# First attention of a graph network: gather indices kept on chip, query rows loaded by SyncE, edge attributes in pairs of groups

## The chip, the cores and the metric

The kernel runs on one NeuronCore of a Trainium2 chip. Its engines are TensorE (PE, with its weight loads PEld), VectorE (DVE), ScalarE (ACT), GpSimd (POOL) and SyncE (SP); each has an instruction queue of its own, and SP, ACT and POOL issue DMAs, which 16 DMA engines carry out. The metric is the device time in microseconds. All arithmetic is in fp32 unless said otherwise.

## The reference, cut to what matters

Four message-passing layers on one graph of 3125 nodes, 64 features and 100,000 edges that are sorted by `dst`, each followed by a residual addition and a layernorm. The change lies in the first one and in its preparation:

```python
Qh, Kh, Vh = (x @ Wq.T + bq), (x @ Wk.T + bk), (x @ Wv.T + bv)     # 3125 x 64, 4 heads of 16
Ee = edge_attr @ We.T + be                                         # 100000 x 64
score = (Kh[src] * Qh[dst] * (1 / sqrt(16)) * Ee).sum(-1)          # per edge and head
score = exp(clip(score, -5, 5))
wV = segment_sum(Vh[src] * score, dst)
x = layernorm(x + wV)
```

## The kernel before, in words

**Tiling.** Edges are cut into G = 98 groups of ST = 1024: 128 partitions (P) by C = 8 columns, partition p of group g holding the edges 8p to 8p+7 of the group. The last group has 84 partitions (PL). Since edges are sorted by `dst`, the destinations of a group fall into a window of W = 64 nodes from a base that is worked out on the chip; a group's rows of queries are fetched with one window and spread to the edges by a one-hot matrix.

**Prologue (L248 to L465).** SyncE and ScalarE load the inputs. `dst_i` (L275, L276) holds every group's destinations in the group layout, so its load is made of pieces of 8 values, 32 bytes. VectorE turns them to fp32 (L370), subtracts each group's base and keeps them as `dst_rel0`. TensorE turns the edge lists (L441), x (L422) and the lowest destinations (L450), and projects x on the weights of K, V and Q: `multiply(k)`, 13 of them, each waiting for ScalarE's copy of the one two before (L315, L316). Among them stands the matmul that spreads the base of every group to all partitions (L459), for which VectorE waits ahead of L378. After the last copy, SyncE stores the K and V rows (`kv_tab`, L287) and ScalarE the Q rows (`q_tab`, L319) to DRAM; the block ends when both have landed.

**First attention (L597 to L857).** One sweep over the 98 groups. Rings of RS = 4 slots hold the gathered K and V rows (`kv`), the edge attributes (`ea`), the indices (`idx`) and the queries (`qwin`). The semaphore `slot_free` starts at 4 and goes up by one with each step's last VectorE instruction (L735). Per step of one group:

- SyncE (`load`, L606) waits for `slot_free`, then loads 4 KB of indices (L544) and 256 KB of edge attributes (L615).
- GpSimd (L630 to L638) issues 8 indirect DMAs, each of 128 rows of 512 bytes from `kv_tab` by one column of `idx`. After the fifth of a group it waits for the indices of the next group (`indices(g + 1)`).
- ScalarE (`front`, L754, and `step`, L777) takes the exponent of the score (L779), then for the next group reads its base into a register and issues two DMAs of 64 query rows into two halves of `qwin` (L761), whose other halves stay zero, copies two transposes out of PSUM (L763, L765), and makes the one-hot of the low part of `src` (L769, L775), for the counting of edges that later layers use.
- TensorE (`step`, L828) counts (L836), turns edge attributes (L794) and one-hots (L802), sums the messages by destination (L851), and multiplies the next group's edge attributes (L811, L813) and queries (L819).
- VectorE (`step`, L690) multiplies keys, edge terms and queries (L704, L712), reduces to the score (L714, L716), adds the counts (L698), makes the one-hots (L676, L683) and the messages (L725), and adds the sum to `acc` (L735).

Each engine's order is written out by hand in these functions; a front half for the next group is woven into each step. The semaphores of the loads count 16 for each finished DMA, whichever number of engines carries it.

After this come a three-hop layer, an attention by matmul, and a last attention with 334 further indirect DMAs on GpSimd (L2282). The change doesn't touch their code.

Of the kernel before, what the change touches and what calls it, by code (L numbers as in the profile page):

```python
# [10 lines left out]
P = 128  # L11
# [55 lines left out]
def build(nc, x, src, dst, edge_attr_2, edge_attr_64, Wq, bq, Wk, bk, We, be, Wv, bv,  # L67
          attn_w, W_fc, W_attn, W_edge, W_e2n, W_m1, W_m2, out):
    ctx = ExitStack()
    with ctx:  # L70
# [86 lines left out]
        g_edge = sb("g_edge", [P, RS, C, D + 4])  # L157
        hot = sb("hot", [P, C, W])
# [27 lines left out]
        def sb(name, shape, dt=fp32):  # L186
# [23 lines left out]
        dst_i = sb("dst_i", [P, G, C], i32)  # L210
# [17 lines left out]
        s_stored = short_sem("tables_stored")  # L228

        early_sems = [s_zero, s_graph, s_gtail, s_x, s_xtail, s_w, s_const, s_edges, s_rest, s_rows, s_tiles, s_flat, s_wt, s_wcopied, s_base, s_basec,  # L230
                      s_bdiag, s_brep, s_sp, s_spt, s_turned, s_copied, s_done, s_taken, s_ones, s_stored]
# [12 lines left out]
        by_pool, by_dve = free_at + 5000, free_at + 7500  # L244

        XT0 = [range(t, min(t + MT, NT)) for t in range(0, NT, MT)]
        MM0 = [range(t, min(t + 2, NT)) for t in range(0, NT, 2)]
        with nc.Block() as block:  # L248
# [12 lines left out]
            def _(sp):  # L261
# [13 lines left out]
                sp.dma_start(dst_i[:, 0:G - 1, :], dst[0:full].rearrange("(g p c) -> p g c", p=P, c=C)).then_inc(s_edges, 16)  # L275
                sp.dma_start(dst_i[0:PL, G - 1, :], dst[full:E].rearrange("(p c) -> p c", c=C)).then_inc(s_edges, 16)  # L276
# [47 lines left out]
            def _(dve):  # L324
                nc.vector.memset(dst_i[:, G - 1, :], int(NONE))
# [43 lines left out]
                dve.wait_ge(s_edges, 32)  # L369
                nc.vector.tensor_copy(dst_rel0[:, :, :], dst_i[:, :, :])  # L370
# [7 lines left out]
                nc.vector.tensor_copy(group_base[:, :], bank[1][:, :])  # L378
                dve.drain()
# [33 lines left out]
                nc.vector.tensor_scalar(tile_hiw[:, :, :], tile_hi[:, :, :], float(WC), 1.0, ALU.mult, ALU.add)  # L413

            @block.tensor
            def _(pe):
# [8 lines left out]
                def multiply(k):  # L425
# [5 lines left out]
                    last.then_inc(s_done, 1)  # L431

# [22 lines left out]
                for k in range(4):  # L455
                    multiply(k)
# [4 lines left out]
                for k in range(4, len(MM0)):  # L461
                    multiply(k)
# [66 lines left out]
        def pass_on(eng):  # L529

            eng.sem_inc(passed, 1)
# [20 lines left out]
        qwin = sb("qwin", [P, RS, 2, D])  # L552
# [33 lines left out]
        slot_free, idx_in = short_sem("a_slot_free"), [short_sem(f"a_idx{s}") for s in range(RS)]  # L586
        ea_in, kv_in = [short_sem(f"a_ea{s}") for s in range(RS)], [short_sem(f"a_kv{s}") for s in range(RS)]
        hot_ok, ea_t, ea_ts, hot_t, hot_ts = short_sem("a_hot"), short_sem("a_eaT"), short_sem("a_eaTs"), short_sem("a_hotT"), short_sem("a_hotTs")
        ee_ok, qd_ok, sc_ok, ex_ok, msg_ok, sum_ok = (short_sem("a_ee"), short_sem("a_qd"), short_sem("a_score"), short_sem("a_exp"), short_sem("a_msg"), short_sem("a_sum"))
        cleared, q_in = short_sem("a_cleared"), short_sem("a_queries")  # L590
# [3 lines left out]
        loop_sems = [begun, slot_free, *idx_in, *ea_in, hot_ok, ea_t, ea_ts, hot_t, hot_ts, ee_ok, qd_ok, sc_ok, ex_ok, msg_ok, sum_ok,  # L594
                     cleared, q_in, key_ok, lo_ok, count_ok, bank_free, count_clear]
        nc.clear_and_free_semaphores(early_sems)
        with nc.Block() as block:  # L597
# [23 lines left out]
            def _(pool):  # L621
                nj = sweeps(pool, 1)
                with pool.Fori(0, nj) as j:
# [7 lines left out]
                    for g in range(G):  # L631
                        s = g % RS
                        for c in range(C):
# [3 lines left out]
                            if c == C // 2 and g + 1 < G:  # L637
                                indices(g + 1)  # L638
# [2360 lines left out]
```

## Time and profile before

| | us |
|---|---|
| median of 3 runs | 1912.07 |
| lowest and highest | 1908.1, 1912.09 |
| span of the profiled execution | 2674.2 |
| prologue, up to the first instruction of the attention's block | 47.2 |
| first gather, last gather issued | 51.75, 1442.83 |
| first gather of the last attention | 1818.4 |

The page gives no time around the span of the profiled execution. The span is from its first to its last instruction, and is longer than the time of the runs. Busy shares of the span: PE 56%, PEld 47%, DVE 53%, ACT 38%, POOL 46%.

How to read a group of instructions: line, engine, operation, tiles written and read, shapes, count; then busy time in us and mean ns of one; then the idle time of the engine right before them, and what ended it. "remote" is a semaphore event that the profile ties to no instruction that had just ended, "issue" is none at all. "PEld" is TensorE's weight load. A "q" behind an engine is its sequencer, which issues DMAs.

### The profile page before, as it was taken

The numbers are of one execution on the slowest core, as the hardware profiler recorded it, in microseconds if no ns is written. First come the engines' busy times: TensorE is split into PE (matmuls) and PEld (weight loads), VectorE is DVE, ScalarE is ACT, GpSimd is POOL, SyncE is SP. The second block draws the span as 40 slices with busy tenths as digits, with TensorE's granted clock in tenths as the row PEclk, the third lists the DMA queues.
The fourth block names the chain that finished last, engine by engine and source line by source line (L and its number), as shares of the span: only waits on it lengthen the run. The fifth ranks groups of instructions, "written<-read, shape, count | busy, mean of one in ns | idle before, by whom it ended". The sixth has DMA issues, their size and how long they took to land. (4 is left out here: it accounts for less than half of the span.)

```text
span 2674.2 us, 43621 instructions
## 1 busy us (share of the span) xinstructions
PE 1501.4 (56%) x12903; PEld 1250.3 (47%) x12903; DVE 1423.4 (53%) x3785; ACT 1008.8 (38%) x2221; POOL 1227.4 (46%) x1328
## 2 busy tenths in 40 slices
PE   3555555555555654555555774754134656555795
PEld 2444444434444443344434673753033645444785
DVE  6455555555555554555555787871023534434685
ACT  3333333333333333333333651750003534434683
POOL 2555555555555554545553460546724343444100
PEclk7677777777777767777777787885556777777897
DMA  5222222222222222222221210022201111111100
GB/s 116 54 58 56 58 59 57 59 57 61 57 58 60 56 59 52 60 55 58 59 57 35 62 59 3 2 87 34 35 17 33 37 34 37 32 41 33 40 26 14
DMA packets 125233, 128.69 MB, mean 48 GB/s; under 512 B 80959, under 2 KB 88435, under 8 KB 124840
## 3 DMA queue, kind: packets, MB, share of 16 engines
q0 software_dynamic: 35776, 62.74, 10.4%
q1 hardware_dynamic: 63778, 57.41, 7.8%
q10 hardware_dynamic: 25542, 6.81, 1.1%
q8 instruction: 75, 1.23, 0.2%
q14 instruction: 62, 0.51, 0.1%
HBM read 116.64 MB, written 10.20 MB: 47 GB/s over the span
## 5 line engine op out<-in xcount | busy, mean ns | idle before, releaser
L634 POOL DMA_INDIRECT shared<-kv_tab,idx x784 | 763.2, 974 | 674.3 <-DMA idx<-in_src 459.3
L836 PE MATMUL bank<-key_hot,lo_hot 128*128 128x350 f16 x784 | 220.8, 394 | 586.5 <-DVE count L698 392.4
L836 PEld LDWEIGHTS bank<-key_hot,lo_hot 128*128 128x128 f16 x784 | 59.3, 101 | 703.4 <-issue 690.4
L2282 POOL DMA_INDIRECT count<-att_tab,count x240 | 228.3, 951 | 301.7 <-PE bank L2827 193.4
L698 DVE TENSOR_TENSOR count<-count,bank 128x350 f32 x392 | 205.4, 524 | 109.4 <-issue 73.6
L735 DVE TENSOR_TENSOR acc<-acc,bank 65x64 f32 x98 | 21.3, 217 | 429.2 <-remote 425.8
L779 ACT ACTIVATE expo<-score 128x32 f32<-128x32 f32 x98 | 22.5, 229 | 587.3 <-DVE score L716 566.9
L769 ACT ACTIVATE lo_dist<-iota_neg,tile_lo 128x128 f16<-128x128 f32 x784 | 238.5, 389 | 0.0
L2656 ACT ACTIVATE shared<-shared 128x126 f32<-128x126 bf16 x336 | 144.4, 484 | 172.0 <-PE bank L2804 88.6
L683 DVE TENSOR_SCALAR key_hot<-iota_key,tile_key 128x350 f16<-128x350 f16 x784 | 193.3, 319 | 0.0
L851 PEld LDWEIGHTS bank<-hots,msg 128*65 128x65 f32 x1568 | 183.8, 221 | 0.4 <-DVE msg L725 0.4
L2804 PE MATMUL bank<-shared 128*128 128x150 f32 x896 | 154.1, 319 | 48.2 <-DVE shared L2509 22.6
L851 PE MATMUL bank<-hots,msg 128*65 128x64 f32 x1568 | 180.4, 303 | 0.0
L2804 PEld LDWEIGHTS bank<-shared 128*128 128x128 f32 x896 | 137.9, 208 | 70.0 <-issue 61.9
L2770 PE MATMUL bank<-shared,ad_row 128*128 128x25 bf16 x1344 | 67.3, 177 | 180.2 <-issue 174.7
L2516 DVE TENSOR_TENSOR count<-count,bank 128x500 f32 x112 | 74.9, 669 | 172.4 <-remote 154.7
L811 PE MATMUL bank<-webd,eaT 128*128 128x128 f32 x784 | 146.3, 345 | 4.2 <-ACT eaT L763 3.5
L2770 PEld LDWEIGHTS bank<-shared,ad_row 128*128 128x128 bf16 x1344 | 51.7, 99 | 196.4 <-issue 195.5
L2838 PE MATMUL bank<-count,tab 128*68 128x88 f32 x1400 | 134.3, 265 | 6.6 <-DVE count L2516 6.5
L811 PEld LDWEIGHTS bank<-webd,eaT 128*128 128x128 f32 x784 | 133.9, 257 | 4.8 <-ACT eaT L763 3.7
L2282 POOL DMA_INDIRECT g_edge<-att_tab,count x94 | 89.0, 946 | 98.6 <-PE bank L2827 71.1
L2838 PEld LDWEIGHTS bank<-count,tab 128*68 128x68 f32 x1400 | 129.9, 162 | 8.6 <-DVE count L2516 8.3
(528 smaller groups left out, 3237.8 us busy)
## 6 DMA issues: line engine op xcount, KB each, us to landing
shared<-in_edge_attr SPq DMA_DIRECT2D x97, 256.0 KB
shared<-lo_tab SPq DMA_DIRECT2D x28, 512.0 KB
shared<-kv_tab,idx POOLq DMA_INDIRECT x784
count<-att_tab,count POOLq DMA_INDIRECT x240
qwin<-q_tab ACTq DMA_DIRECT2D x196, 16.0 KB
kv_tab<-count SPq DMA_DIRECT2D x1, 1600.0 KB, 10.4
idx<-in_src SPq DMA_DIRECT2D x97, 4.0 KB, 1.6
g_edge<-att_tab,count POOLq DMA_INDIRECT x94
```

The costliest lines, as they stand in the source:

```text
L634: nc.gpsimd.indirect_dma_start(kv[:, s, c, :], None, kv_tab, bass.IndirectOffsetOnAxis(ap=idx[:, s, c:c + 1], axis=0)).then_inc(kv_in[s], 16)
L683: last = nc.vector.tensor_scalar(key_hot[:, c, :], iota_key[:, :], keys[:, c:c + 1], None, ALU.is_equal)
L698: nc.vector.tensor_tensor(at, at, bank[6 + q % 2][:, 0:KC].rearrange("p (h w) -> p h w", w=WC), ALU.add).then_inc(bank_free, 1)
L769: nc.scalar.activation(lo_dist[:, c, :], iota_neg[:, :], ACT.Abs, bias=los[:, c:c + 1])
L811: nc.tensor.matmul(bank[3][:, q * P:(q + 1) * P], eaT[:, q * P:(q + 1) * P], webd[:, :], start=q == 0, stop=False, skip_group_check=True)
L836: last = nc.tensor.matmul(bank[6 + q % 2][:, 0:KC], lo_hot[:, c, :], key_hot[:, c, :], start=i == 0, stop=i == GT - 1)
L851: last = nc.tensor.matmul(bank[5][0:D + 1, 0:W], msg[:, c, :], hots[:, s % 2, c, :], start=c == 0, stop=c == C - 1)
L2282: nc.gpsimd.indirect_dma_start(ring[s][:, j, 0:D + 2], None, att_tab[1], bass.IndirectOffsetOnAxis(ap=src_i[:, t:t + 1], axis=0)).then_inc ...
L2656: nc.scalar.activation(low_w[:, n % LOW_RING, 0:FREE], low_dist[:, n % LOW_RING, 0:FREE], ACT.Relu, bias=p, scale=minus_p).then_inc(low_ok, 1)
L2770: last = nc.tensor.matmul(bank[0][:, t * NT:(t + 1) * NT], lo_turned[:, s, t, :], u_parts[:, k, :], start=k == 0, stop=k == 2)
L2804: nc.tensor.matmul(into[:, 0:NT * QW].rearrange("p (h w) -> p h w", w=QW)[:, :, bass.ds(at[j], TW)], low_w[:, n % LOW_RING, :], keys_w[:, ...
L2838: last = nc.tensor.matmul(sum_of[0:D + 4, 0:UW], tab[:, h, 0:D + 4], blocks[:, i % 2, h, :], start=h == 0, stop=h == NT - 1, skip_group_ch ...
```

## The change

The index ring and the waits for it go. In the prologue `dst` and `src` are each loaded as 98 rows of 1024 values, one group to a partition (`dst_g`, `src_g`; 97 rows in one DMA, the rest in another), made fp32 by VectorE, turned by TensorE in 8 transposes each (`turn_groups`), and copied by VectorE to `dst_rel0` and, as integers, to `idx_all`, which lies in memory that the first attention doesn't use (`g_edge`). GpSimd gathers by columns of `idx_all` and waits for `slot_free` ahead of each group. SyncE loads a step's 64 query rows to both halves of the partitions (`q_raw`); ScalarE copies each half to its place in a single `qwin`. Two groups' edge attributes come in one DMA, except for the last two groups.

```diff
-        dst_i = sb("dst_i", [P, G, C], i32)
+        dst_g, dst_gf = sb("dst_g", [P, ST], i32), sb("dst_gf", [P, ST])
...
+        def turned_groups(b):
+            return bank[b][:, 0:C // 2 * G].rearrange("p (c g) -> p c g", c=C // 2)
...
             @block.sync
-                sp.dma_start(dst_i[:, 0:G - 1, :], dst[0:full].rearrange("(g p c) -> p g c", p=P, c=C)).then_inc(s_edges, 16)
-                sp.dma_start(dst_i[0:PL, G - 1, :], dst[full:E].rearrange("(p c) -> p c", c=C)).then_inc(s_edges, 16)
+                for into, of in ((dst_g, dst), (src_g, src)):
+                    sp.dma_start(into[0:G - 1, :], of[0:full].rearrange("(g e) -> g e", e=ST)).then_inc(s_edges, 16)
+                    sp.dma_start(into[G - 1:G, 0:E - full], of[full:E].rearrange("(a e) -> a e", a=1)).then_inc(s_edges, 16)
...
             @block.vector
-                nc.vector.memset(dst_i[:, G - 1, :], int(NONE))
+                nc.vector.memset(dst_g[:, :], int(NONE))
+                nc.vector.memset(src_g[:, :], 0)
...
-                dve.wait_ge(s_edges, 32)
-                nc.vector.tensor_copy(dst_rel0[:, :, :], dst_i[:, :, :])
+                dve.wait_ge(s_edges, 64)
+                nc.vector.tensor_copy(dst_gf[0:G, :], dst_g[0:G, :])
+                nc.vector.tensor_copy(src_gf[0:G, :], src_g[0:G, :])
+                dve.drain().then_inc(s_dstg, 1)
                 dve.wait_ge(s_basec, 1)
...
                 nc.vector.tensor_copy(group_base[:, :], bank[1][:, :])
+                dve.wait_ge(s_dstt, 1)
+                for k in range(2):
+                    nc.vector.tensor_copy(dst_rel0[:, :, k * C // 2:(k + 1) * C // 2], turned_groups(2 + 5 * k).rearrange("p c g -> p g c"))
...
+                dve.wait_ge(s_srct, 1)
+                for k in range(2):
+                    nc.vector.tensor_copy(idx_all[:, k * C // 2:(k + 1) * C // 2, :], turned_groups(3 + k))
...
             @block.tensor
-                for k in range(4):
+                for k in range(2):
+                    multiply(k)
+                pe.wait_ge(s_dstg, 1)
+                turn_groups(dst_gf, 2, 7, s_dstt)
+                for k in range(2, 4):
                     multiply(k)
                 pe.wait_ge(s_bdiag, 1)
...
-                for k in range(4, len(MM0)):
+                for k in range(4, 6):
+                    multiply(k)
+                turn_groups(src_gf, 3, 4, s_srct)
+                for k in range(6, len(MM0)):
                     multiply(k)
...
             @block.sync
+                    def load_queries(g, s):
+                        b = spans(sp, g)
+                        sp.dma_start(q_raw[:, s, :], q_tab[bass.ds(b, W), :].rearrange("(a w) f -> a w f", a=1).to_broadcast([2, W, D])).then_inc(q_in[s], 16)
+
                     def load(g, s, m):
...
+                        if both and s % 2 == 0:
+                            sp.wait_ge(slot_free, j * G + g + 2)
+                            pass_on(sp)
+                            sp.dma_start(ea[:, s:s + 2, :], ea_main[bass.ds(g, 2), :, :].rearrange("g p n -> p g n")).then_inc(ea_in[s // 2], 16)
...
+                        load_queries(g, s)
+
+                    sp.wait_ge(begun, j + 1)
+                    pass_on(sp)
                     each(sp, load)
             @block.gpsimd
-                    indices(0)
                     for g in range(G):
                         s = g % RS
+                        pool.wait_ge(slot_free, j * G + (g + 1))
+                        pass_on(pool)
                         for c in range(C):
                             nc.gpsimd.indirect_dma_start(
-                                kv[:, s, c, :], None, kv_tab, bass.IndirectOffsetOnAxis(ap=idx[:, s, c:c + 1], axis=0)
+                                kv[:, s, c, :], None, kv_tab, bass.IndirectOffsetOnAxis(ap=idx_all[:, c, g:g + 1], axis=0)
                             ).then_inc(kv_in[s], 16)
-                            if c == C // 2 and g + 1 < G:
-                                indices(g + 1)
             @block.scalar
-                        b = spans(act, g)
+                        act.wait_ge(q_in[s], (j * uses(s) + m) * 16)
+                        pass_on(act)
                         for i in range(2):
-                            act.dma_start(qwin[i * W:(i + 1) * W, s, i, :], q_tab[bass.ds(b, W), :]).then_inc(q_in, 16)
+                            last = nc.scalar.activation(qwin[i * W:(i + 1) * W, i, :], q_raw[i * W:(i + 1) * W, s, :], ACT.Copy)
+                        last.then_inc(q_put, 1)
             @block.tensor
-                        pe.wait_ge(q_in, n * 32)
+                        pe.wait_ge(q_put, n)
```

## Rows read from the trace of the kernel before

**Rows 1.** Page, part 5 (columns as in the section above): three groups of the first attention.

```profile
L634 POOL DMA_INDIRECT shared<-kv_tab,idx x784 | 763.2, 974 | 674.3 <-DMA idx<-in_src 459.3
...
L735 DVE TENSOR_TENSOR acc<-acc,bank 65x64 f32 x98 | 21.3, 217 | 429.2 <-remote 425.8
L779 ACT ACTIVATE expo<-score 128x32 f32<-128x32 f32 x98 | 22.5, 229 | 587.3 <-DVE score L716 566.9
```

**Rows 2.** Timeline: start us, length us, engine, line, tiles, count, [idle before <-releaser].

```profile
616.50 0.60 ACT L763 ACTIVATE eaT<-bank 128x512 f32<-128x512 f32 x1 [1.68 <-issue]
...
618.08 1.93 PE L851 MATMUL bank<-hots,msg 128*65 128x64 f32 x16
...
623.19 0.22 DVE L735 TENSOR_TENSOR acc<-acc,bank 65x64 f32 x1 [2.57 <-remote]
...
623.63 0.33 SPq L544 DMA_DIRECT2D idx<-in_src  x1
...
626.08 0.95 POOL L634 DMA_INDIRECT shared<-kv_tab,idx  x1 [4.29 <-DMA idx<-in_src]
```

**Rows 3.** Timeline of the last steps of the first attention.

```profile
1442.83 0.95 POOL L634 DMA_INDIRECT shared<-kv_tab,idx  x1 [0.30 <-issue]
...
1454.02 0.21 DVE L735 TENSOR_TENSOR acc<-acc,bank 65x64 f32 x1
...
1463.15 0.21 DVE L735 TENSOR_TENSOR acc<-acc,bank 65x64 f32 x1
...
1465.04 0.76 PE L836 MATMUL bank<-key_hot,lo_hot 128*128 128x350 f16 x4 [1.40 <-ACT lo_hot L775]
...
1466.02 0.53 DVE L698 TENSOR_TENSOR count<-count,bank 128x350 f32 x1
```

**Rows 4.** Windows: stretch, its us, busy of PE, PEld, DVE, ACT, POOL, clock, DMA.

```profile
51.70:1443.80 1392.10, 763.08 (x4688) 588.61 (x4688) 744.65 (x1838) 476.30 (x1153) 763.25 (x784) 0.73 0.23 58
```

**Rows 5.** Line L2282: ns min/median/max, first to last start us, forms.

```profile
L2282 POOL DMA_INDIRECT count<-att_tab,count x240: 942/947/1498, 1818.4 to 2425.4; - x120
L2282 POOL DMA_INDIRECT g_edge<-att_tab,count x94: 942/947/994, 1919.4 to 2497.4; - x94
```

**Rows 6.** Timeline of the prologue and of the attention's start.

```profile
5.45 0.40 SPq L275 DMA_DIRECT2D dst_i<-in_dst  x1
...
7.47 2.14 DVE L340 MEMSET count<- 128x2500 int32 x1 [0.47 <-issue]
...
13.62 4.68 PE L441 MATMUL bank<-ident,count 128*128 128x128 f32 x21
...
23.42 0.57 DVE L370 CAST dst_rel<-dst_i 128x784 f32<-128x784 int32 x1
...
24.73 0.39 ACT L315 ACTIVATE count<-bank 128x256 f32<-128x256 f32 x1 [1.67 <-PE bank L430]
...
34.57 0.22 ACT L316 ACTIVATE shared<-bank 128x64 f32<-128x64 f32 x1
...
48.20 2.73 DVE L648 MEMSET count<- 128x3200 int32 x1 [10.77 <-issue]
...
51.75 1.14 POOL L634 DMA_INDIRECT shared<-kv_tab,idx  x1 [45.56 <-DMA idx<-in_src]
```

**Rows 7.** Waits of SyncE's queue, 600 to 1200 us: total us, times, longest.

```profile
SPq L531 <- DVE acc L735: 519.5, 40, 20.5
```

**Rows 8.** DMA queues (packets, MB, share of 16 engines): 2667:2675, 1425:1436, 600:1200.

```profile
q1 hardware_dynamic: 1350, 0.34, 17.0%
...
q1 hardware_dynamic: 196, 0.17, 6.5%
...
q10 hardware_dynamic: 6720, 1.38, 1.1%
```

**Rows 9.** DMA: all packets of 48.1:50, then GpSimd's queue of 600:1200.

```profile
DMA packets 257, 0.76 MB, mean 398 GB/s; under 512 B 16, under 2 KB 16, under 8 KB 257
...
q0 software_dynamic: 10752, 22.04, 14.7%
```

More of the change, by code:

```diff
@@ L157, in build @@
         g_edge = sb("g_edge", [P, RS, C, D + 4])
+        edge_words = g_edge[:, :, :, :].rearrange("p s c f -> p (s c f)")
+        idx_all = edge_words[:, 0:G * C].bitcast(i32).rearrange("p (c g) -> p c g", c=C)
+        src_g, src_gf = edge_words[:, 0:ST].bitcast(i32), edge_words[:, ST:2 * ST]
         hot = sb("hot", [P, C, W])
@@ L431, in multiply, with turn_groups @@
                     last.then_inc(s_done, 1)
+                def turn_groups(of, first, second, turned):
+                    for c in range(C):
+                        last = nc.tensor.transpose(bank[first if c < C // 2 else second][:, c % (C // 2) * G:(c % (C // 2) + 1) * G],
+                                                   of[0:G, :].rearrange("g (p c) -> g c p", c=C)[:, c, :], ident[0:G, 0:G])
+                    last.then_inc(turned, 1)
                 pe.wait_ge(s_const, 4)
@@ L604, in _ @@
                     pass_on(sp)
+                    def load_queries(g, s):
+                        b = spans(sp, g)
+                        sp.dma_start(q_raw[:, s, :], q_tab[bass.ds(b, W), :].rearrange("(a w) f -> a w f", a=1).to_broadcast([2, W, D])).then_inc(q_in[s], 16)
                     def load(g, s, m):
[L607 to L615 removed]
+                        both = not isinstance(g, int)
+                        if both and s % 2 == 0:
+                            sp.wait_ge(slot_free, j * G + g + 2)
+                            pass_on(sp)
+                            sp.dma_start(ea[:, s:s + 2, :], ea_main[bass.ds(g, 2), :, :].rearrange("g p n -> p g n")).then_inc(ea_in[s // 2], 16)
+                        elif not both:
+                            sp.wait_ge(slot_free, j * G + g + 1)
+                            pass_on(sp)
+                            if g == G - 1:
+                                sp.dma_start(ea[0:PL, s, :], ea_last).then_inc(ea_end, 16)
+                            else:
+                                sp.dma_start(ea[:, s, :], ea_main[g, :, :]).then_inc(ea_in[s // 2], 16)
+                        load_queries(g, s)
+                    sp.wait_ge(begun, j + 1)
+                    pass_on(sp)
                     each(sp, load)
@@ L789, in turn_edges @@
                     def turn_edges(g, s, m):
-                        pe.wait_ge(ea_in[s], (j * uses(s) + m) * 16)
+                        if isinstance(g, int) and g == G - 1:
+                            pe.wait_ge(ea_end, (j + 1) * 16)
+                        else:
+                            pe.wait_ge(ea_in[s // 2], (j * ea_loads[s // 2] + m) * 16)
                         pass_on(pe)
```

35 lines of the change are left out of this document (13 added, 22 removed).

## Prediction

> **What bounds the kernel now.** I read the page first, for the span and the engines. The profiled execution spans 2674.2 us, while the median of the runs is 1912.07 us: it is 762 us longer. Its rows give durations and order, but its steps are longer than those of a plain run, so I price the change from rows and add it to the median.
>
> The groups of the first attention come next [rows 1]. GpSimd issues 784 gathers (98 steps of 8), 974 ns each, and idled 459 us for the index load; VectorE idled 426 us ahead of its last addition (L735); ScalarE idled 567 us for VectorE's score. Everybody waits for somebody, so the timeline of one step must say who is last. There [rows 2] TensorE's matmuls of L851, whose semaphore releases L735, end at 620.0, yet L735 starts at 623.2: the release came 3 us after the work. Once the last gather is out, at 1443.8, this lag is gone: L735 stands at 1454.02 and at 1463.15 [rows 3], a step of 9.1 us, against 14.2 us for the mean of the 98 steps of the gather stretch, 1392.1 us long [rows 4]. The late release goes with gathers in the profiled execution.
>
> How long is a step in a plain run? If it were 14.2 us, 98 steps would leave 520 of 1912 us. But the last attention alone issues 334 gathers of 947 ns [rows 5], 0.30 us apart like those of [rows 3]: 418 us. And the stretches without gathers are 52 us ahead of the first [rows 6], 375 us from 1443.8 to 1818.4 and 176 us behind the last [rows 5]. That doesn't fit. GpSimd's own pace nearly does: 8 x (0.974 + 0.30) = 10.2 us a step, 999 us in all, and the sum is 52 + 999 + 375 + 418 + 176 = 2020 us, within 6% of the median. So I take **GpSimd's issue of gathers, 10.2 us a step**, as the bound, with the chain over VectorE and TensorE, 9.1 us, close behind. The 4.3 us that GpSimd waits for indices in the profiled step [rows 2] are an effect, not a cause: the index load of 623.63 was itself let go by L735. GpSimd is three groups ahead there and waits for room.
>
> **The parts in the loop.** *Indices kept on chip.* 98 loads of 4 KB leave SyncE's queue. GpSimd waits for the free slot ahead of a group instead of for the indices after the fifth gather of the group before: one wait for one wait, and the 8 gathers cost the same. When GpSimd sets the pace neither wait stops it. Gain per step: 0, with 0.3 us to either side as bounds, one gap between gathers.
>
> *Query rows.* ScalarE loses two DMA issues and a register load (together with the slot's wait, 1.68 us ahead of L763, [rows 2]) and gets two copies of 64 columns, by the nearest row 0.22 us each [rows 6], 0.45 together: 1.2 us less on ScalarE. But ScalarE idles 5.8 us a step for the score (567 / 98, [rows 1]), and the copy that follows (L763, done at 617.1) is used behind L851, which ends at 620.0 [rows 2]. Value 0; if that cover were gone, the saving would be the 1.2 us. SyncE gets a register load and an issue of about 0.33 us as L544's [rows 2], and nothing is behind it: its queue waited for L735 for 520 of 600 us [rows 7].
>
> *Edge attributes.* One load of 512 KB for two groups starts a step later than now, still three steps, 27 us, ahead of use. An index load needed 2.4 us from issue to use (623.63 to 626.08, [rows 2]); the larger load adds 1.3 us at 398 GB/s [rows 9]. Hidden by two steps.
>
> *Start of the loop.* The first gather starts at 51.75, released by an index load; VectorE, which frees the slots, starts at 48.20 [rows 6]. The gather would then start near 48.4: **3.3 us less**, which counts in full if GpSimd sets the pace. SyncE now waits for the base rows before it loads edge attributes, so step 0 begins later by a load, 2.4 to 3.7 us; GpSimd has four groups of room then, 41 us, and doesn't notice.
>
> **The prologue.** This is where the time moves. The load of dst in 12,416 pieces of 32 bytes becomes two loads, of dst and of src, each of 97 rows of 4096 bytes into 97 partitions. VectorE waits for both ahead of its casts, and TensorE, in the middle of the projections, waits for the casts.
>
> How many of the 16 DMA engines carry such a load? Count packets [rows 8]. At the end of the kernel SyncE's queue stores 1280 rows and then 53 rows of 256 bytes, and shows 1350 packets: 1280 + 53 leaves 17, a closing packet for each of 16 engines and *one* for the 53 rows. The last index and edge loads, of 84 rows each, show 196: 2 x 84 + 2 x 14. ScalarE's 84 loads of 64 rows show 6720: 84 x (64 + 16). So 64 rows take 16 engines, 84 take 14, 53 take one: the largest number up to 16 that divides the rows. 97 is prime, as 53 is: **one engine** carries each load, and the second queues behind the first.
>
> The Trainium skill, DMA: Bandwidth & Descriptors, section "Why a DMA increments its semaphore by 16 and not by 1", states such a rule (the number must divide the slowest dimension of both sides) and, for another way of issuing, an exception that spreads 127 partitions over all engines. By the rule the sum is the one below, by the exception rival A's; no row here has 97 partitions.
>
> Rate of one engine: where large packets run alone, 398 GB/s by 16, or 24.9 GB/s, so 397 KB take 16.0 us; by the gathers' packets, 22.04 MB in 14.7% of 16 x 600 us, 15.6 GB/s and 25.5 us [rows 9]. I take the first: these are plain contiguous rows with the engine nearly to themselves. Two memsets of 1024 columns, 0.88 us each by 2.14 for 2500, stand ahead of SyncE's tail loads, so the first load is issued at 5.45 + 1.7 = 7.15 [rows 6]; two loads take 32.0; with 2.4 from issue to use, the casts start at 41.6. VectorE arrives there at 23.4 and doesn't wait now.
>
> From there: two casts of 1024 columns, 0.74 each by 0.57 for 784, to 43.1; eight transposes at 0.22 (4.68 for 21), to 44.9; the first projection, 0.75, and ScalarE's copies of the 11 projections left, 0.77 each (13 between 24.73 and 34.79, base matmuls included), 8.5; the eight transposes of src, 1.8, of which 0.3 hides behind those copies: 55.7. Now the copies end at 34.8 [rows 6]. The store of the tables follows as now. So **+20.9 us**. VectorE's own work behind the base matmuls (8.8 us, plus four copies of 392 columns) stays beside the stores.
>
> Sum: 1912.1 + 20.9 - 3.3 + 98 x 0 = **1930 us**. Bounds: with 25.5 us a load, +19, 1949; with no wait for the loads at all, the casts (less L370) and the transposes remain, 0.9 + 3.6 - 3.3 = +1, 1913. Both ends are kept.
>
> **Rivals.** *A, the loads are spread* over many engines (10%). Against it, the packet counts. Then it is 1913, or slightly less, since 12,416 small packets no longer stand beside the weights: no change.
>
> *B, the step is set by ScalarE's part* and falls (15%, faster). The place is from the exponent to the one-hots (L779 to L775), for which TensorE's count matmul waits. If this is last in a plain run, each step gains up to 1.2 us, 118 us in all: 1812. It decides from 17.6/98 = 0.18 us a step on; with 0.3 us it is 1900. Against it: in the tail, without any lag, L836 waits for L775 until 1465.04, but VectorE's addition that needs it starts at 1466.02, right behind VectorE's own work [rows 3]. And a faster chain gains nothing while GpSimd needs 10.2.
>
> *C, the wait for indices is a real stall* (5%, faster). The 459 us are 4.7 a step; a tenth of them would give 1884. Against it: the slot's release let the load go.
>
> *D, the loop gets slower* (4%): the double edge load is late once in two steps, 1 us each time, 1979. It decides only if 3.7 us don't fit into three steps.
>
> **How the numbers follow.** The forecast has 66% and 1913 to 1949 as its own range. The range given, 1893 to 1949, adds A and the near part of B and leaves out the rest of B, C and D. About 0.2%, 4 us, is what a measurement of this kernel can tell from no change. Faster: B and C, 0.20. Same: A, 0.10. Slower: the forecast and D, 0.70.
>
> **What the profile after would show.** VectorE idle some 17 us ahead of the casts, released by a DMA; TensorE idle between the second and third projection; the stores issued near 56; the first gather near 69; GpSimd waiting for L735's line where it waited for the index load; a tail step near 9 us. It would be wrong if the casts stood before 30, or if the 8 gathers of a step took less than 10 us. If the median falls though the prologue grew, a plain run's step was not set by GpSimd.

## The result, and the profile after

| | median us | lowest to highest | runs |
|---|---|---|---|
| before | 1912.02 | 1908.1 to 1923.3 | 6 |
| after | 1928.84 | 1918.53 to 1934.17 | 6 |

The ratio of after to before is 1.0076, 95% interval 1.0049 to 1.0103: 16.8 us slower by the medians, where 17.6 us (1930) were forecast. The ratios in this document come from the single runs and aren't the quotient of the two medians (1.0088 here).

The page of after, first line of its head and three groups of the first attention. The first and the third answer to [rows 1]; the second is VectorE's multiplication by the gathered keys. The line numbers have moved (L634 is L676, L704 is L744, L779 is L821, L735 is L775).

```profile
span 1916.7 us, 43354 instructions
...
L676 POOL DMA_INDIRECT shared<-kv_tab,g_edge x784 | 763.0, 973 | 303.1 <-issue 300.9
...
L744 DVE TENSOR_TENSOR prod<-bank,shared 128x512 f32<-128x512 f32 x98 | 67.8, 692 | 135.8 <-DMA shared<-kv_tab,g_edge 116.6
...
L821 ACT ACTIVATE expo<-score 128x32 f32<-128x32 f32 x98 | 22.5, 229 | 217.0 <-DVE score L756 180.1
```

This profiled execution took 1918.53 us, the lowest of its six. Its span fits its time, as the 2674.2 us of the kernel before did not. Of GpSimd's 303.1 idle us 64.4 lie ahead of its first gather, 2.1 us in seven waits for VectorE's L775, and the rest is the 0.30 us between one gather and the next; VectorE waits for the gathers' DMA. So GpSimd is the engine that ends last in the loop. The waits for index loads and for L735 that filled [rows 1] are gone, and the experiments show that they had been peculiar to that one execution.

The prologue of after, from the timeline (start us, length us, engine, line, names, idle before and releaser). It answers to [rows 6].

```profile
7.07 0.42 SPq L284 DMA_DIRECT2D dst_g<-in_dst  x1
7.54 4.49 SPq L285 DMA_DIRECT2D dst_g<-in_dst  x1
...
12.06 0.90 SPq L284 DMA_DIRECT2D g_edge<-in_src  x1
...
13.01 15.06 SPq L285 DMA_DIRECT2D g_edge<-in_src  x1
...
41.77 0.69 DVE L380 CAST dst_gf<-dst_g 98x1024 f32<-98x1024 int32 x1 [17.37 <-DMA g_edge<-in_src]
42.38 0.69 DVE L381 CAST g_edge<-g_edge 98x1024 f32<-98x1024 int32 x1
...
43.16 1.57 PE L454 MATMUL bank<-ident,dst_gf 98*128 98x98 f32 x8 [16.71 <-DVEq L382]
...
56.55 0.22 ACT L325 ACTIVATE shared<-bank 128x64 f32<-128x64 f32 x1
...
56.80 0.42 SPq L296 DMA_DIRECT2D kv_tab<-count  x1
...
70.20 2.73 DVE L688 MEMSET count<- 128x3200 int32 x1 [9.22 <-issue]
...
70.60 1.14 POOL L676 DMA_INDIRECT shared<-kv_tab,g_edge  x1 [64.44 <-issue]
```

VectorE stands idle for 17.37 us until the load of src has landed, and TensorE for 16.71 us behind it. The store of the tables is issued at 56.80, right behind ScalarE's last copy at 56.55; in [rows 6] that copy stands at 34.57. The first gather starts at 70.60, against 51.75.

What the DMA engines moved in that wait, from 14 to 41 us of after, in 40 equal slices: busy tenths of 16 engines, then GB/s.

```profile
DMA  0000000000000000000000013000000111010000
GB/s 24 30 24 24 30 24 24 30 24 24 24 30 24 24 24 30 24 22 30 24 24 30 24 25 33 24 24 24 30 24 24 31 45 49 35 43 24 30 24 24
```

33 of the 40 slices show 24 to 30 GB/s, nearly all with a busy share under a tenth. One engine of 16 is 6% of them, and the prediction's estimate of its rate was 24.9 GB/s. That fits both loads going through one engine, one behind the other; the experiments test it.

### The profile page after: what moved, and what is told of

Read it like the earlier page. It is cut to its first block and busy times, and to the rows that moved or that the text cites. A ratio compares the mean times of both kernels' runs of the same rounds, so it can differ in the third digit from the quotient of the medians.

```text
span 1916.7 us, 43354 instructions
## 1 busy us (share of the span) xinstructions
PE 1357.8 (71%) x12919; PEld 1149.2 (60%) x12919; DVE 1419.6 (74%) x3791; ACT 1069.7 (56%) x2417; POOL 1239.5 (65%) x1328
## 3 DMA queue, kind: packets, MB, share of 16 engines
q0 software_dynamic: 35776, 62.74, 13.7%
## 5 line engine op out<-in xcount | busy, mean ns | idle before, releaser
L676 POOL DMA_INDIRECT shared<-kv_tab,g_edge x784 | 763.0, 973 | 303.1 <-issue 300.9
L881 PE MATMUL bank<-key_hot,lo_hot 128*128 128x350 f16 x784 | 189.0, 347 | 295.1 <-DVE count L738 200.9
L2849 PE MATMUL bank<-shared 128*128 128x150 f32 x896 | 158.0, 325 | 22.2 <-DVE shared L2530 17.6
L744 DVE TENSOR_TENSOR prod<-bank,shared 128x512 f32<-128x512 f32 x98 | 67.8, 692 | 135.8 <-DMA shared<-kv_tab,g_edge 116.6
L807 ACT ACTIVATE hotT<-bank 128x512 f32<-128x512 f32 x98 | 58.5, 597 | 176.4 <-PE bank L847 176.4
L896 PE MATMUL bank<-hots,msg 128*65 128x64 f32 x1568 | 151.3, 270 | 0.0
L896 PEld LDWEIGHTS bank<-hots,msg 128*65 128x65 f32 x1568 | 150.9, 187 | 0.4 <-DVE msg L765 0.4
L821 ACT ACTIVATE expo<-score 128x32 f32<-128x32 f32 x98 | 22.5, 229 | 217.0 <-DVE score L756 180.1
L817 ACT ACTIVATE lo_hot<-lo_dist,small 128x1024 f16<-128x1024 f16 x98 | 112.5, 1148 | 25.4 <-issue 25.3
L2883 PE MATMUL bank<-count,tab 128*68 128x88 f32 x1400 | 112.1, 240 | 9.3 <-DVE count L2561 9.1
L2883 PEld LDWEIGHTS bank<-count,tab 128*68 128x68 f32 x1400 | 107.5, 140 | 11.9 <-DVE count L2561 11.8
L864 PE MATMUL bank<-qwin,hotT 128*128 128x128 f32 x784 | 113.5, 288 | 0.0
```

The costliest lines, as they stand in the source:

```text
L676: nc.gpsimd.indirect_dma_start(kv[:, s, c, :], None, kv_tab, bass.IndirectOffsetOnAxis(ap=idx_all[:, c, g:g + 1], axis=0)).then_inc(kv_in[ ...
L864: last = nc.tensor.matmul(bank[4][:, c * D:(c + 2) * D], hotT[:, c // 2, :], qwin[:, :, :].rearrange("p a f -> p (a f)"), start=True, stop ...
L881: last = nc.tensor.matmul(bank[6 + q % 2][:, 0:KC], lo_hot[:, c, :], key_hot[:, c, :], start=i == 0, stop=i == GT - 1)
L896: last = nc.tensor.matmul(bank[5][0:D + 1, 0:W], msg[:, c, :], hots[:, s % 2, c, :], start=c == 0, stop=c == C - 1)
L2849: nc.tensor.matmul(into[:, 0:NT * QW].rearrange("p (h w) -> p h w", w=QW)[:, :, bass.ds(at[j], TW)], low_w[:, n % LOW_RING, :], keys_w[:, ...
L2883: last = nc.tensor.matmul(sum_of[0:D + 4, 0:UW], tab[:, h, 0:D + 4], blocks[:, i % 2, h, :], start=h == 0, stop=h == NT - 1, skip_group_ch ...
```

## The experiments

Twelve experiments were run, on ten edited kernels; one of these and the kernel before were each run a second time. The kernel before ran beside each of the four batches: 1912.69, 1910.75, 1912.32 and 1912.14 us median.

### The loads cut into 96 rows and one

```diff
-sp.dma_start(into[0:G - 1, :], of[0:full]...)
+sp.dma_start(into[0:G - 2, :], of[0:full - ST]...)
+sp.dma_start(into[G - 2:G - 1, :], of[full - ST:full]...)
-dve.wait_ge(s_edges, 64)
+dve.wait_ge(s_edges, 96)
```

> The changed kernel, but each of the two long loads is cut into 96 rows and one row, so that 96 rows can go over 16 DMA engines. Theory (one engine carried the 97 rows): both loads land before VectorE asks for them near 24.4 us, its 17.4 us of idle time ahead of the casts vanish, and of the prologue's growth only casts and transposes stay: about 17 us less than the changed kernel, 1912 +-4. Rival (the loads are slow for their bytes or for their 4096-byte rows, not for the number of engines): the casts stay near 41 us and the time near 1929.

1907.14 us (12 runs), ratio to before 0.9978, interval 0.996 to 0.9996: 21.7 us less than after. The timeline:

```profile
7.07 0.43 SPq L284 DMA_DIRECT2D dst_g<-in_dst  x1
...
7.54 0.26 SPq L285 DMA_DIRECT2D dst_g<-in_dst  x1
...
24.48 0.69 DVE L381 CAST dst_gf<-dst_g 98x1024 f32<-98x1024 int32 x1
...
36.89 0.22 ACT L326 ACTIVATE shared<-bank 128x64 f32<-128x64 f32 x1
...
50.93 1.14 POOL L677 DMA_INDIRECT shared<-kv_tab,g_edge  x1 [44.77 <-issue]
```

The same bytes, cast and turned by the same instructions, now cost no wait: the casts start as soon as VectorE is free, 17.3 us earlier than in after, the last copy 19.7 and the first gather 19.7 us earlier. 97 rows in one load are the cause of the loss, and the casts and the transposes are not; that it isn't the loop is shown below. SyncE's queue, blocked for 4.49 and 15.06 us in after, is free at once.

It came out 5 us below the 1912 that were expected, just outside the 4 us allowed, so it ran again later:

> The version whose loads are cut into 96 rows and one row, a second time: it measured 0.998 of before. By the prediction's own sum without the wait it should be 1 us over before, 1912; if the 3.6 us below were real, 1907 again. Theory: first gather 0.9 us earlier than before and the rest the same, so 1909 to 1911, ratio 0.998 to 1.000; rival: 1905 to 1908, ratio under 0.998.

1906.87 us (12 runs), ratio 0.9975, interval 0.9962 to 0.9988: again 5 us below before, on the rival's side of what I had written. The version is faster than both kernels. Where its 5 us come from is taken up with the clock, below.

### One of the two loads only

```diff
+if of is dst:
     sp.dma_start(into[0:G - 1, :], ...)
+else:
+    sp.dma_start(into[0:G - 2, :], ...)
+    sp.dma_start(into[G - 2:G - 1, :], ...)
-dve.wait_ge(s_edges, 64)
+dve.wait_ge(s_edges, 80)
```

> Only dst is still loaded as 97 rows; src is cut into 96 rows and one row. Theory (each 97-row load takes one engine for 16.0 us, and the second queued behind the first): issued at 7.1, a load of 16.0 us and up to 2 us for what else that engine carries end at 25 to 27, the casts start at 25 to 27.5 instead of 24.5 (both cut) and 41.8 (none cut), and the time is 1 to 3 us over the version with both cut, 1908 to 1911. Rival (the two loads do not add, each is slow in itself because of its waiting or its issue, which blocked SyncE): casts at 41, time 1927 to 1930. SyncE should be blocked by no issue for more than 5 us.

1914.82 us (12 runs), ratio 1.002, interval 1.0005 to 1.0035. The timeline of its casts:

```profile
28.05 0.69 DVE L384 CAST dst_gf<-dst_g 98x1024 f32<-98x1024 int32 x1 [3.17 <-DMA g_edge<-in_src]
```

The casts start 3.4 us later than with both loads cut (24.65 in its twin, the second run of the version above, in the same batch) and 13.7 us earlier than with none cut. So the two loads do add, and the rival, that each is slow in itself, falls. SyncE's longest issue took 4.42 us, behind the load of dst, as expected under 5. The casts came 0.5 us after the end of the bracket. The releaser named is src, so the rows of src that fall to the engine of dst probably queue behind it; that wasn't tested by itself. The time was 4 to 7 us above what I expected. The first gather stood 6.3 us later than in the twin (57.37 against 51.10), though the casts were only 3.4 us late. The windows from 29 to 35 us, this kernel first and then its twin, show the rest (stretch, its us, busy of PE, PEld, DVE, ACT, POOL, granted clock, DMA share, GB/s):

```profile
29.00:35.00 6.00, 5.57 (x24) 5.57 (x25) 1.91 (x6) 1.11 (x4) 0.00 (x0) 0.55 0.01 3
29.00:35.00 6.00, 6.00 (x40) 5.40 (x40) 4.72 (x9) 3.37 (x13) 0.00 (x0) 1.00 0.02 4
```

TensorE had stood idle for 2.50 us ahead of the transposes of dst, and did the work behind them at a granted clock of 0.55 instead of 1.00: 8 projections took 2.82 us instead of 1.49, and the base matmuls 1.92 instead of 1.06.

### The new prologue with the old loop

The kernel before, with the loads, casts, transposes and memsets of after; src is turned, but the loop loads its indices as before.

```diff
-sp.dma_start(dst_i[:, 0:G - 1, :], ...)
+for into, of in ((dst_g, dst), (src_g, src)):
+    sp.dma_start(into[0:G - 1, :], ...)
...
+turn_groups(dst_gf, 2, 7, s_dstt)
...
+turn_groups(src_gf, 3, 4, s_srct)
```

> The kernel before with the new prologue alone: both long loads, casts, transposes and copies as in the change, but the loop loads its indices, queries and edge attributes as before (the turned indices are made and not used). Theory (all of the loss is in the prologue, the loop gives back only its earlier first gather): 21 to 22 us over the kernel before, 1933, that is 3 to 4 us over the changed kernel. Rival (the loop part of the change costs or saves something per step): the difference to the changed kernel is clearly other than 3 to 4 us, by 98 times what a step gained or lost.

1930.34 us (6 runs), ratio 1.0111, interval 1.0078 to 1.0144. That is 1.5 us over after, within the spread of both, where 3 to 4 were expected. The prologue holds the whole loss. The gathers of this kernel and of after, by line (ns min/median/max, first to last start us):

```profile
L666 POOL DMA_INDIRECT shared<-kv_tab,idx x784: 940/944/2202, 73.9 to 1075.2; - x196
```

```profile
L676 POOL DMA_INDIRECT shared<-kv_tab,g_edge x784: 940/944/2322, 70.6 to 1071.2; - x196
```

The part of the change in the loop lets the gathers start 3.3 us earlier, as predicted, and then both kernels need the same time for them: 1001.3 and 1000.6 us, 10.2 us for a step of 8.

### Two sweeps instead of one

One line in either kernel makes the whole loop run twice, so the difference to the kernel of one sweep is the price of a loop without its prologue.

```diff
-nc.vector.tensor_scalar(sweeps_i[:, 1:2], sweeps_f[:, 2:3], 1.0, None, ALU.add)
+nc.vector.tensor_scalar(sweeps_i[:, 1:2], sweeps_f[:, 2:3], 2.0, None, ALU.add)
```

> The kernel before with one more sweep over all 98 groups in the first attention, which adds nothing to the sums. Its extra time, divided by 98, is the length of a step in a plain run. Theory (GpSimd's issue sets the pace, 10.2 us): 1000 to 1030 us more, with the sweep's own start in it. Rival C (the wait for indices is a real stall of 4 us a step): 1390 us more. Rival B (ScalarE's part decides): 1000 to 1120, and clearly more than the same edit gives to the changed kernel.

> The changed kernel with one more sweep over all 98 groups of the first attention, which adds nothing to the sums. Theory (GpSimd's issue of 784 gathers sets the pace before and after): the extra time is the same as the extra sweep's in the kernel before, to within 10 us (0.1 us a step), 1000 to 1030. Rivals B and C: it is less than before by up to 118 or by up to 400 us. If SyncE's later loads slow a step down, it is more.

2932.32 us (before) and 2945.58 us (after), 4 runs each: a sweep costs 1019.6 and 1016.7 us more than one sweep did. The loop of after is 2.9 us cheaper over 98 steps, 0.03 us a step, which the measurement can't tell from nothing. The gathers of the two kernels, by line:

```profile
L634 POOL DMA_INDIRECT shared<-kv_tab,idx x1568: 940/944/2202, 51.8 to 2071.9; - x196
```

```profile
L676 POOL DMA_INDIRECT shared<-kv_tab,g_edge x1568: 940/945/2310, 75.6 to 2094.5; - x196
```

2020.1 and 2018.9 us for 1567 intervals are 1.289 and 1.288 us each, with the pause between the sweeps in them.

### Half of the gathers

The pace of the gathers could hide a gain in the rest of the step. So each step gathers only for the first four of its eight chunks of edges; the output leaves out the other half of the edges.

```diff
-for c in range(C):
+for c in range(C // 2):
     nc.gpsimd.indirect_dma_start(
...
-dve.wait_ge(kv_in[s], m * (16 * C))
+dve.wait_ge(kv_in[s], m * (8 * C))
```

> The kernel before with 4 of 8 gathers in each step of the first attention; half of the keys and values are zeros, so its output leaves out half of the edges. GpSimd then needs 5.1 us a step, and what is behind it shows. Theory: the chain over VectorE and TensorE, 9.0 to 9.5 us a step, becomes the bound: 70 to 115 us under 1912, so 1797 to 1842. If a step takes no less time, GpSimd was not the bound.

> The changed kernel with 4 of 8 gathers in each step of the first attention; its output leaves out half of the edges. Theory: again 9.0 to 9.5 us a step. ScalarE's saved 1.2 us a step is off the chain, so it stands 14 to 22 us over the same edit on the kernel before, the prologue's loss (a little more than in the full kernel, since an earlier first gather counts less when VectorE sets the pace). Rival B (ScalarE's part is next in line): it gains up to 1.2 us a step on that kernel and stands under it.

1839.83 and 1847.29 us (4 runs each). Half of the gathers taken away saves 71 us in one kernel and 82 in the other, 0.7 to 0.8 us a step of the 5 us that GpSimd is relieved of: the other engines' step stands only 1 us behind GpSimd's. (The edit also zeroes, once, the half of `kv` that isn't gathered.) The groups of GpSimd in the two, 200 to 1000 us:

```profile
L642 POOL DMA_INDIRECT shared<-kv_tab,idx x330 | 323.1, 979 | 449.0 <-DMA idx<-in_src 365.9 <-issue 83.1
```

```profile
L684 POOL DMA_INDIRECT shared<-kv_tab,g_edge x337 | 343.2, 1018 | 434.7 <-DVE acc L784 352.0 <-issue 82.6
```

Here GpSimd does wait, for the index load in the old loop and for VectorE's addition in the new one, one wait for one wait. The additions, by line:

```profile
L744 DVE TENSOR_TENSOR acc<-acc,bank x98: 198/207/214, 90.3 to 994.9; 65x64 f32 x98
```

```profile
L784 DVE TENSOR_TENSOR acc<-acc,bank x98: 202/208/216, 110.0 to 1004.6; 65x64 f32 x98
```

904.6 and 894.6 us for 97 steps are 9.33 and 9.22 us. Relieved of half of the gathers, the new loop is 0.1 us a step faster, 10 us in all, and of the 16.8 us that the change costs only 7.5 remain. I had expected 14 to 22. Which part of the change gives the 0.1 us isn't shown by a run of its own. From 200 to 1000 us VectorE waits for no gather's DMA in either kernel, so it isn't the index load's wait that it was freed of. Its waits for TensorE's matmuls of the edge attributes (total us, times, longest), half of the gathers before and after, from 200 to 1000 us:

```profile
DVE prod L713 <- PE bank L822: 32.7, 26, 1.7
```

```profile
DVE prod L753 <- PE bank L867: 24.1, 22, 1.9
```

The 8.6 us between them are 0.1 us a step. That would fit ScalarE's shorter part: rival B in small, a tenth of its 1.2 us, and only where the gathers don't set the step.

### The transposes behind the projections

Both loads cut, the memsets reduced to the ends of the last two rows, and all transposes of dst and src moved behind the last projection, out of the way of the store. VectorE casts dst where it did, and src after its copy of the bases; its work on the other tables comes ahead of that on dst.

```diff
-nc.vector.memset(dst_g[:, :], int(NONE))
+nc.vector.memset(dst_g[G - 2:G, E - (G - 1) * ST:ST], int(NONE))
...
-for k in range(2):
-    multiply(k)
-pe.wait_ge(s_dstg, 1)
-turn_groups(dst_gf, 2, 7, s_dstt)
-for k in range(2, 4):
+for k in range(4):
     multiply(k)
...
-for k in range(4, 6):
+for k in range(4, len(MM0)):
     multiply(k)
+pe.wait_ge(s_dstg, 2)
+turn_groups(dst_gf, 2, 7, s_dstt)
 turn_groups(src_gf, 3, 4, s_srct)
-for k in range(6, len(MM0)):
-    multiply(k)
```

> The changed kernel with its loads cut into 96 rows and one, with memsets of 352 instead of 1024 columns, and with all transposes of dst and src behind the last projection, where the stores of the tables hide them; VectorE's work on the other tables comes before that on dst. Theory: nothing of the change is left on the prologue's path and the first gather is still earlier by about 3.5 us: 1908 to 1909, faster than both. Rival (TensorE's transposes were hidden anyway, or VectorE's chain behind them now outlasts the stores): no better than the kernel with the loads cut alone, 1912 or more.

1910.52 us (12 runs), ratio 0.9983, interval 0.9962 to 1.0003, between the 1908 to 1909 of the theory and the 1912 of the rival. In its profiled execution the store was issued at 35.41 and the first gather at 49.21, 1.7 us earlier than in the first version, yet it isn't faster, and between the two no difference is shown. Its last addition of the loop stood at 1062.9, that of the first version at 1063.7, and what followed took 846.7 against 839.8 us.

### The kernel before once more, and the clock

> The kernel before, not edited, as a measure of the noise and for a second profiled execution. The profiled span of 2674.2 us was either that one execution's own (theory: the span is then 1905 to 1915, the steps of the attention 10.2 us, the first gather near 51.8 and the last addition of a step near 1064), or it belongs to this kernel under the profiler (rival: 2600 to 2750 again, steps of 14.2 us). The ratio to before should be 1 within 0.2%.

1912.5 us (12 runs), ratio 1.0005, interval 0.999 to 1.0019. The profiled span is 1910.4 us, and the loop has no wait for an index load in 200 to 1000 us:

```profile
L634 POOL DMA_INDIRECT shared<-kv_tab,idx x627 | 610.1, 973 | 191.1 <-issue 191.1
```

So the stretched steps of [rows 2] and [rows 4] belonged to that one execution; what stretched it stays open. The estimate of 10.2 us a step, made against them, is what a plain execution shows. The span came as expected; the first gather (58.17 for 51.8) and the last addition (1069.4 for 1064) did not. The prologue of this execution:

```profile
5.89 9.41 SPq L276 DMA_DIRECT2D dst_i<-in_dst  x1
...
28.00 1.91 PE L459 MATMUL bank<-lowest_diag,ones 128*128 128x128 f32 x8
...
29.70 11.09 PE L430 MATMUL bank<-wcat,count 65*128 65x192 f32 x34
...
41.25 0.40 SPq L287 DMA_DIRECT2D kv_tab<-count  x1
...
58.17 1.14 POOL L634 DMA_INDIRECT shared<-kv_tab,idx  x1 [51.98 <-DMA idx<-in_src]
```

This isn't the prologue that the prediction read. The last 34 projections took 11.09 us and not the 6.72 of that execution, and the first gather stood at 58.17 and not at 51.75. The windows show at which clock (columns as above):

```profile
19.00:24.00 5.00, 3.33 (x25) 2.23 (x24) 4.69 (x9) 3.13 (x7) 0.00 (x0) 1.00 0.05 10
24.00:29.00 5.00, 5.00 (x21) 4.71 (x21) 1.56 (x5) 2.21 (x8) 0.00 (x0) 0.60 0.00 0
29.00:35.00 6.00, 6.00 (x22) 6.00 (x21) 4.82 (x8) 1.66 (x6) 0.00 (x0) 0.50 0.01 3
35.00:41.00 6.00, 6.00 (x21) 5.52 (x19) 1.61 (x4) 2.93 (x11) 0.00 (x0) 0.50 0.00 1
```

TensorE was busy for 3.33 of the 5 us from 19 to 24, and then it was granted 0.60 on the mean of 24 to 29 and 0.50, the lower level of 1.2 GHz, for the rest of the projections. In the execution that the prediction read, the clock stayed at 1.00:

```profile
19.00:24.00 5.00, 3.77 (x27) 2.52 (x26) 4.75 (x10) 3.40 (x7) 0.00 (x0) 1.00 0.05 10
24.00:29.00 5.00, 5.00 (x33) 4.49 (x31) 2.65 (x7) 2.72 (x10) 0.00 (x0) 1.00 0.00 0
29.00:35.00 6.00, 5.68 (x29) 4.12 (x28) 5.36 (x10) 4.29 (x17) 0.00 (x0) 1.00 0.02 4
```

It had been busy for 3.77 us from 19 to 24 there. But that stretch alone doesn't decide it. In the kernel with the transposes behind the projections TensorE was busy no longer than where the clock fell, and the clock stayed:

```profile
19.00:24.00 5.00, 3.30 (x26) 2.07 (x23) 4.78 (x9) 3.40 (x7) 0.00 (x0) 1.00 0.00 0
24.00:29.00 5.00, 5.00 (x33) 4.69 (x34) 2.83 (x7) 2.21 (x8) 0.00 (x0) 1.00 0.00 0
```

What decides it isn't shown. Of the four profiled executions of this prologue (before, before again, two sweeps, half gathers) two went each way: 51.8, 51.8, 58.2 and 58.2 us to the first gather.

After, TensorE sits idle for 16.71 us and comes back at the lower clock:

```profile
28.00:41.00 13.00, 0.00 (x0) 0.00 (x0) 0.00 (x0) 0.00 (x0) 0.00 (x0) 0.53 0.10 30
41.00:47.00 6.00, 3.85 (x16) 3.85 (x17) 2.86 (x7) 0.55 (x2) 0.00 (x0) 0.50 0.01 1
47.00:53.00 6.00, 6.00 (x36) 5.71 (x35) 3.35 (x6) 2.53 (x10) 0.00 (x0) 0.82 0.01 3
53.00:57.00 4.00, 3.35 (x18) 2.42 (x16) 3.87 (x6) 2.83 (x12) 0.00 (x0) 1.00 0.01 2
```

In this execution the clock rose near 49. In the kernel of after with two sweeps it stayed at 0.50 from 41 to 62 us, through all of the projections, and the first gather stood at 75.6 instead of 70.6. Where both loads are cut there is no such idle time, and the clock was 1.00 from 19 to 35 us in all three profiled executions. Two experiments tried to hold the clock.

```diff
+pe.wait_ge(s_flat, 1)
+for k in range(3):
+    nc.tensor.transpose(bank[2][:, k * P:(k + 1) * P], ident[:, :], ident[:, :])
 pe.wait_ge(s_base, 1)
```

> The kernel before with three transposes of the unit matrix, whose result nobody reads, in TensorE's pause of 0.6 to 1.0 us between the transposes of x and those of the lowest rows. In four profiled executions of this prologue the granted clock behind that pause was 1.00 twice (table store at 34.8, first gather at 51.8) and 0.50 twice (41.3 and 58.2). Theory (the half clock in the projections is what the prologue of before loses in about half of its executions, 6.4 us each time): clock 1.00 from 24 to 35 us, first gather at 51.8 to 52.2, median 2 to 4 us under before, 1908.5 to 1910.5. Rival (the clock falls whatever TensorE does there): store at 41, first gather at 58, or a median equal to before within 1 us.

1911.82 us (12 runs), ratio 0.9995, interval 0.9982 to 1.0008. In the one profiled execution the clock was 1.00 from 22 to 35 us, the store at 34.09 and the first gather at 51.04, and yet the median didn't fall by the 2 to 4 us. Either the clock mostly stays at 1.00 here when no profile is taken, or what the prologue gains is lost again behind the loop: there this execution took 848.0 us, and the one of the kernel before with its first gather at 58.17 took 840.7. So the end of the run doesn't follow the first gather one to one, and why is open. Behind the last addition of the loop all kernels with one or two full sweeps run the same code, and in their profiled executions (the stretched one aside) it took between 836.5 us (after) and 848.9 us (before, two sweeps).

This leaves the 5 us open by which the version with both loads cut is faster than before: its first gather (50.93 and 51.10) stands where it stands here, and here nothing was gained. What does differ is the granted clock over the whole execution, which every run lists, profiled or not: 0.840 as the mean of the 24 runs of that version, 0.835 for the 52 runs of before beside them, 0.836 here. Among the runs of before the long ones tend to be those with the lower clock (1906.98 us at 0.837, 1921.37 at 0.830). But the kernel with the transposes behind the projections had 0.840 too, and 1910.52 us. So clock and time go together in part, and no run shows that the clock makes the 5 us.

```diff
+for k in range(68):
+    nc.tensor.transpose(bank[2][:, k % 4 * P:(k % 4 + 1) * P], ident[:, :], ident[:, :])
 pe.wait_ge(s_dstg, 1)
```

> The kernel after with 68 transposes of the unit matrix, whose result nobody reads, while TensorE waits for the casts of the 97-row loads (16.7 us of idle time; 68 of 0.22 us are 15.0). In the two profiled executions of after the projections behind that idle time ran at the lower clock until 49 or throughout, and the first gather stood at 70.6 and 75.6. Theory (idle time on TensorE makes the wait for the loads dearer than its own length, by 2.4 to 7.4 us): casts at 41.8 as before, granted clock 1.00 from 43 on, table store at 54 to 55, first gather at 68 to 69, median 2 to 7 us under after, 1922 to 1927, and 13 to 16 us over before. Rival (the clock makes no difference to the time): 1929 within 1.5 us.

1926.11 us (5 runs), ratio 1.007, interval 1.0053 to 1.0086: inside the theory's 1922 to 1927, but no difference to after that the intervals tell. Nor can the number speak for the theory, since the edit didn't make its own condition, as its timeline shows:

```profile
27.22 9.14 PE L483 MATMUL bank<-ident 128*128 128x128 f32 x68
...
43.17 1.57 PE L454 MATMUL bank<-ident,dst_gf 98*128 98x98 f32 x8 [6.81 <-DVEq L382]
```

The 68 transposes took 9.14 us and not 15.0: 0.134 us each, against 0.22 in the group of 21 from which I had priced them, though that group ran at a clock of 1.00 and shows no idle time either. It took 3.61 to 4.75 us in the profiled executions, and why isn't shown. TensorE still idled 6.81 us, the clock was 0.50 from 41 to 60 us, and the first gather stood at 75.5. The theory wasn't tested by it.

## Why the prediction was right, point by point

**The direction, the place and the size.** 1928.84 against 1930. All of the loss is in the prologue (the old loop behind the new prologue costs the same), and cutting the two loads takes it away, with 5 us to spare. That the sum came within 1.2 us is in part luck: the first gather stood at 51.8 or 58.2 us with the prologue of before, and at 70.6 or 75.6 with that of after, from one profiled execution to the next, and the prediction had read one of these courses.

**One DMA engine for 97 rows.** Confirmed by 24 to 30 GB/s in the wait, by 96 rows and one row, which cost no wait, and by cutting only one of the loads, which took away 13.7 of the 17.3 us. This was the step that decided: with the loads spread, as in rival A, the cut version shows that the result would have been under before. The Trainium skill, DMA: Bandwidth & Descriptors, section "Why a DMA increments its semaphore by 16 and not by 1", gives the rule of the divisor; the trace agrees, with 97 rows on one engine, and the exception for another way of issuing didn't apply here.

**The terms.** The first load issued at 7.15, measured 7.07. Casts at 41.6, measured 41.77, for two loads of 16.0 us, one behind the other, and 2.4 us to use; the three terms were not measured apart. Casts until 43.1, measured 43.07. VectorE idle some 17 us, measured 17.37. Last copy at 55.7, measured 56.77: the step that was short by 1.1 us is the projections behind the casts, priced by rows at the higher clock; eight of them took 2.81 us at the lower one and 1.62 where it rose. The first gather near 69, measured 70.60 and, where the clock stayed low, 75.6.

**The base of the prologue.** The prediction took the store at 34.8 as the prologue of before. That was one of two courses; with the other, the change costs 15.6 and not 22.0 us up to the store (56.80 less 41.25 or 34.81). Between the means of the profiled executions, 55.0 of four for before and 72.3 of three for after (70.6, 70.6 and 75.6), the first gather moved by 17.3 us. That lies near the 16.8 us measured, but since holding the clock in the kernel before brought nothing, it isn't shown that the two belong together.

**The loop.** Gain per step 0, with 0.3 us either way as bounds: 0.03 measured, at 10.2 us a step. That GpSimd's own pace sets the step was right, and it was found against the profile's own steps of 14.2 us. The sum of 2020 us that supported it was 108 us too long mainly because the stretches without gathers were stretched too: 375 us between the attentions and 176 at the end, against 353 and 64 in the plain execution of before. The chain over VectorE and TensorE, put at 9.1 us, showed as steps of 9.3 and 9.2 us with half of the gathers; a tail step near 9 us isn't there in after, where only the last step stands behind the last gather, and it took 7.8 us (1072.18 to 1080.01). Start of the loop 3.3 us earlier: 3.3 in the trace, of which the runs show 1.5, not separable from nothing. The statement that GpSimd would wait for L735's line where it had waited for the index load was wrong for the kernel itself, where these waits come to 2.1 us in 784 gathers; it came true only with half of the gathers.

**The rivals.** A fell: the loads aren't spread. B fell at its full price; the 0.1 us a step that appears with half of the gathers may be a remnant of it. C fell: the waits for indices don't exist in a plain execution. D fell: over a sweep the loop with the double edge load is no slower than the other.

## What to carry to other kernels

Count the rows of a load before its bytes: 97 rows of 4 KB, one engine and 34.7 us for two loads; 96 rows and one row, no wait at all. A resource that a kernel waits for in one profiled execution need not be what it waits for in the median run. Where span and time differ, work out each step from the durations of single instructions, and test the sum against the time. And a wait on TensorE's path in a prologue is priced too low by its length alone if the matmuls behind it may run at the lower clock: 3.4 us late at the casts stood as 6.3 us at the first gather.

## What the runs showed of the hardware

While a slow load is being served, the queue that issued it can be held up in its next issues: SyncE stood for 4.49 and 15.06 us in the issues behind the 97-row loads, and for 9.41 us in the one behind the load of 12,416 pieces of 32 bytes before the change; with both loads cut no issue of an edge load took over 0.43 us.

The granted clock took two courses with the same program. TensorE's work ahead of the two courses differed by 0.44 us from 19 to 24, and the 34 projections behind took 6.72 us at 1.00 or 11.09 us at 0.50. In another kernel as little work in that stretch (3.30 us) was followed by 1.00. With nothing but transposes on TensorE (27.2 to 36.4 us of the last experiment) the granted clock was 0.50 up to 30, 0.94 from 30 to 33 and 1.00 from 33 on; after the idle time behind them it was 0.50 again from 41.

A profiled execution can be longer than the run it stands for by 762 us, with a gather at its usual length (974 ns against 973) and late releases between the engines; of the fourteen profiled executions in this study one was so.
